# A fused gather-sum and MLP kernel: the three layers and the transposes of each step one quad earlier in TensorE's order

## Chip, cores and metric

The kernel runs on one NeuronCore of a Trainium2 chip. The metric is the device time of one execution in microseconds, the median of several. Everything is float32.

## The reference, cut to what matters

There are 12,500 nodes with 128 features (`x`) and 200,000 edges with 128 features. Edges are sorted by their destination `dst`; `src` takes no part in the result.

```python
h   = relu(layernorm(x))                                   # no affine part
agg = segment_sum(edge_attr, dst, num_segments=12500)      # [12500, 128]
u   = relu(concat([h, agg]) @ W1 + b1)
u   = relu(u @ W2 + b2)
y   = u @ W3 + b3
out = x + layernorm(y) * ln_w + ln_b
```

## The kernel before

**Units of work.** A chunk is 384 edges (128 partitions, 3 edges each), a quad is 4 chunks (1,536 edges, 768 KB), and there are 130 full quads and a tail chunk. A group is 384 nodes (3 per partition); there are 32 full groups and a last one of 212 nodes. A step handles four quads (k = 0 to 3) and one group; there are 31 steps, after six quads that run ahead (AHEAD = 6). All edges of a group must have been summed before its first layer needs the sums; step i computes group i after the quads up to 4i + 4 have been added.

**A quad.** SyncE loads it into one of eight slots of `ring` in two DMAs (L293), each reload waiting until the segment sum that used the slot is done. VectorE writes one-hot matrices for two quads at a time (`make_onehot`, L862). TensorE's `seg` (L422) multiplies one-hots and edges, 12 calls that show as 24 matmuls, into `part_ps`, two banks by turns. ScalarE copies the result to `part` (`copy_part`, L639). GpSimd builds a placement matrix (`placement`, L784), which may run one quad ahead of `put`. TensorE's `put` (L433) multiplies the two into `place_ps`; it handles the quad before the one just summed. VectorE's `add` (L938) adds that to `agg` at a base read from a table.

**A group.** VectorE takes statistics of x (`stats_x` L835, `mean_x` L843), ScalarE the root (`x_sqrt` L645), VectorE the reciprocal and shift (`scale_x` L850, `shift_x` L855), ScalarE writes h (`normalise` L653) and GpSimd adds ln_b to x (`bias_x` L792) once h is written. TensorE transposes h (`transpose_h` L442), ScalarE copies that to `h_t` (`copy_ht` L662). Layer 1 is a product of h (`layer1_x` L450) and one of the sums (`layer1_sums` L457, which waits for `added`); ScalarE's `relu1` (L669), then layer 2 (L467), `relu2` (L675), then layer 3 (L473), six matmuls into the single bank `y_ps`. VectorE empties it (`take_y` L943), takes statistics (`stats_y` L963, `mean_y` L971), centers in three instructions (`center_y` L979), and after ScalarE's `y_sqrt` (L681) does `scale_y` (L987) and `output` in three instructions (L997), and SyncE stores the group. `layer3(g)` waits for `y_evacuated`, which `take_y(g - 1)` signals.

**What sets the order.** Each engine runs its own program in order, written out by hand in a function `step` per engine; semaphores join them. The order in `step` is what the change edits, for TensorE, ScalarE and VectorE. GpSimd's step (`rows_of`, four placements, `bias_x(i + 1)`) and SyncE's (a load of x, four reloads) are untouched. The last two groups and the last quads are written out behind the loop on each engine (from `q, g = QUADS - 4, GROUPS - 2`). Most of the output stores are issued by SyncE only after its last load. A first part of the program checks that the fast path fits the data; this one always takes it.

Of the kernel before, what the change touches and what calls it, by code (L numbers as in the profile page):

```python
# [70 lines left out]
AHEAD = 6  # L71
# [5 lines left out]
def gnn_kernel(nc, x, dst, edges, w1, b1, w2, b2, w3, b3, lnw, lnb, out):  # L77
    assert GROUPS == 32 and QUADS == 4 * STEPS + AHEAD and LAST_P * LAST_PER == LAST_N and RC * RP == REST
    with ExitStack() as ctx:
# [73 lines left out]
        x_loaded = [sem("x_loaded_even"), sem("x_loaded_odd")]  # L153
# [116 lines left out]
        with nc.Block() as block:  # L270
# [113 lines left out]
            def _(pe):  # L384
# [75 lines left out]
                def layer1(g, sums=None):  # L460
                    layer1_x(g)
                    layer1_sums(g, sums)
# [32 lines left out]
                def fast():  # L495
                    pe.wait_ge(wts_loaded, WTS)
                    for q in range(AHEAD):
                        if q >= 2:
                            pe.wait_ge(part_copied, q - 1)
                            seg(q, q, LANDED, q // 2 + 1)  # L500
                        if q >= 1:
                            put(q - 1, q - 1, free=q >= 3)
                    transpose_h(0)

                    def step(i, par, pairs):


                        for k in range(4):
                            turn_q = 4 * par + AHEAD + k
                            q = 4 * i + AHEAD + k  # L510
                            seg(q, turn_q, LANDED * (pairs + turn_q // RING + 1),
                                2 * i + AHEAD // 2 + k // 2 + 1 if k % 2 == 0 else None)
                            put(q - 1, turn_q - 1)
                            if k == 0:
                                layer1(i, 4 * i + AHEAD - 1)
                            elif k == 1:
                                layer2(i)
                            elif k == 2:
                                layer3(i)
                            else:  # L520
                                transpose_h(i + 1)

                    step(0, 0, 0)
                    with pe.Fori(0, (STEPS - 3) // 2) as t:
                        step(2 * t + 1, 1, t)
                        step(2 * t + 2, 0, t + 1)
                    step(STEPS - 2, 1, (STEPS - 2) // 2)

                    q, g = QUADS - 4, GROUPS - 2

                    def loads_of(quad):
                        return LANDED * (quad // RING + 1)

                    layer1_x(g)
                    seg(q, q, loads_of(q), q // 2 + 1)
                    put(q - 1, q - 1)
                    layer1_sums(g, q - 1)
                    put(q, q)  # L540
                    transpose_h(g + 1)
                    seg(q + 1, q + 1, loads_of(q + 1))
                    layer2(g)
                    put(q + 1, q + 1)
                    layer1_x(g + 1)
                    seg(q + 2, q + 2, loads_of(q + 2), q // 2 + 2)
                    layer3(g)
                    put(q + 2, q + 2)
                    seg(q + 3, q + 3, loads_of(q + 3))
                    layer1_sums(g + 1, QUADS - 1)  # L550
                    put(q + 3, q + 3)
                    slot = QUADS % RING
                    pe.wait_ge(onehot_ready, QUADS // 2 + 1)
                    pe.wait_ge(edges_loaded[slot], loads_of(QUADS) - LANDED + 16)
                    for j in range(PER):
                        last = nc.tensor.matmul(part_ps[QUADS % 2][0:WIN, 0:D], onehot[:, (QUADS // 2) % 2, 0, j, :],
                                                ring[:, slot, j * D:(j + 1) * D], start=(j == 0), stop=(j == PER - 1))
                    last.then_inc(seg_done, 1)
                    layer2(g + 1)
                    layer1_x(LAST)  # L560
                    put(QUADS, QUADS, rows=WIN)
                    layer3_last_bias()
                    layer3(g + 1)
                    layer1_sums(LAST, QUADS + 1)
                    layer2(LAST)
                    layer3_last()
# [49 lines left out]
            def _(act):  # L616
# [71 lines left out]
                def fast():  # L688
                    act.wait_ge(wts_loaded, WTS)
                    for q in range(2):  # L690
                        copy_part(q, q)
                    x_sqrt(0)
                    normalise(0)
                    for q in range(2, AHEAD):
                        copy_part(q, q)
                    copy_ht(0)

                    def step(i, first=False, more_x=False):
                        q = 4 * i + AHEAD
                        copy_part(q, AHEAD)  # L700
                        relu1(i)
                        x_sqrt(i + 1)
                        copy_part(q + 1, AHEAD + 1)
                        relu2(i)
                        normalise(i + 1)
                        copy_part(q + 2, AHEAD + 2)
                        if not first:
                            y_sqrt(i - 1)
                        copy_part(q + 3, AHEAD + 3)
                        copy_ht(i + 1)  # L710
                        if more_x:
                            x_sqrt(i + 2)
                            normalise(i + 2)

                    step(0, first=True)
                    with act.Fori(1, STEPS - 2) as i:
                        step(i)
                    step(STEPS - 2, more_x=True)

                    q, g = QUADS - 4, GROUPS - 2  # L720
                    copy_part(q, q)
                    relu1(g)
                    copy_ht(g + 1)
                    copy_part(q + 1, q + 1)
                    relu2(g)
                    y_sqrt(g - 1)
                    copy_part(q + 2, q + 2)
                    copy_part(q + 3, q + 3)
                    relu1(g + 1)
                    y_sqrt(g)  # L730
                    copy_part(QUADS, QUADS, rows=WIN)
                    relu2(g + 1)
                    relu1(LAST)
                    relu2(LAST)
                    y_sqrt(g + 1)
                    act.wait_ge(y_centered, g + 2)
                    act.wait_ge(y_rstd_done, g + 2)
                    for j in range(PER):
                        nc.scalar.activation(z[:, j, :], z[:, j, :], ACT.Copy, scale=y_rstd[:, j:j + 1]).then_inc(z_scaled, 1)
                    y_sqrt(LAST)  # L740
                    act.wait_ge(full_out_ready, PER)
                    act.dma_start(group_rows(out, g + 1), xg(g + 1)).then_inc(stored, 16)
# [87 lines left out]
            def _(dve):  # L830
# [179 lines left out]
                def fast():  # L1010
# [8 lines left out]
                    base = bases(0, AHEAD - 1)  # L1019
# [8 lines left out]
                    def step(i, par, pairs, first=False, more_x=False):  # L1028

                        make_onehot(2 * i + 4, 0)
                        base = bases(4 * i + AHEAD - 1, 4)
                        q = 4 * i + AHEAD - 1
                        add(q, 1, base[0])
                        stats_x(i + 1, x_loaded[1 - par], 16 * (pairs + par) + 16)
                        if not first:
                            take_y(i - 1)
                        add(q + 1, 0, base[1])  # L1040
                        mean_x(i + 1)
                        if not first:
                            stats_y(i - 1)
                        scale_x(i + 1)
                        shift_x(i + 1)
                        if not first:
                            mean_y(i - 1)
                        add(q + 2, 1, base[2])
                        if not first:
                            center_y(i - 1)  # L1050
                        make_onehot(2 * i + 5, 1)
                        if more_x:
                            stats_x(i + 2, x_loaded[par], 16 * pairs + 32)
                            mean_x(i + 2)
                        add(q + 3, 0, base[3])
                        if more_x:
                            scale_x(i + 2)
                            shift_x(i + 2)
# [14 lines left out]
                    add(q - 1, q - 1, base[0])  # L1073
                    stats_y(g - 1)
                    mean_y(g - 1)
                    add(q, q, base[1])
                    center_y(g - 1)
                    make_onehot(q // 2 + 2, 1)
                    add(q + 1, q + 1, base[2])
                    scale_y(g - 1)  # L1080
                    output(g - 1)
                    add(q + 2, q + 2, base[3])
                    take_y(g)
                    stats_y(g)
                    mean_y(g)
                    center_y(g)
                    scale_y(g)
# [83 lines left out]
```

## Time and profile before

| | |
|---|---|
| median of 3 runs | 320.87 us (320.09 to 321.0) |
| the profiled execution | 320.3 us |
| its span in the profile | 318.4 us |
| TensorE matmul busy | 273.7 us |
| VectorE busy | 246.2 us |
| GpSimd busy | 179.5 us |
| ScalarE busy | 149.8 us |
| bytes moved by DMA | 116.49 MB, mean 366 GB/s |
| mean granted TensorE clock | 0.977 |

The span runs from the first to the last recorded event, the execution's own time has a little around it. Busy is the time in which an engine ran at least one data instruction. The shares are means over a start of some 30 us, 31 steps and a tail of some 20 us, and each of these has a limit of its own.

### The profile page before, as it was taken

To read this page: it belongs to the slowest core of one execution; us is meant where nothing else is said; L and a number is where in the kernel's file an instruction comes from. 1 tells how busy PE (TensorE), PEld (TensorE's weight loads), DVE (VectorE), ACT (ScalarE), POOL (GpSimd) and SP (SyncE) were. 2 spreads that over 40 slices of the span, in tenths; PEclk is the share of its full clock that TensorE was granted. 3 is DMA by queue.
4 is the path that set the end of the run, shared out by engine and by line. 5 is a ranking of instruction groups with operands and counts; after the bars stand their busy time and mean duration, and the time that the engine had idled before them with its cause. 6 is when DMAs were issued, how large, how long until landed. Compare 5 with 4: busy or idle time off the path is not lost.

```text
span 318.4 us, 12666 instructions
## 1 busy us (share of the span) xinstructions
PE 273.7 (86%) x3927; PEld 186.3 (58%) x3927; DVE 246.2 (77%) x944; ACT 149.8 (47%) x407; POOL 179.5 (56%) x208
## 2 busy tenths in 40 slices
PE   2959998998988787999888888898888888898991
PEld 0736666665655555666556565565556565566560
DVE  4946588988778787588787977777787977777984
ACT  1542555555444444455444555544445555545632
POOL 8636555666545565266565665555565665555531
PEclk9977999999999999899999999999999999999997
DMA  7999999999999999999999999999999999999994
GB/s 245 344 379 371 373 371 372 373 386 373 386 373 379 381 373 386 373 374 372 373 373 373 373 374 372 373 373 373 373 373 373 373 373 373 373 373 374 376 399 158
DMA packets 81534, 116.49 MB, mean 366 GB/s; under 512 B 5392, under 2 KB 81520, under 8 KB 81520
## 3 DMA queue, kind: packets, MB, share of 16 engines
q1 hardware_dynamic: 80506, 115.86, 103.3%
q10 hardware_dynamic: 1014, 0.46, 0.5%
q8 instruction: 7, 0.11, 0.1%
q14 instruction: 7, 0.06, 0.1%
HBM read 109.90 MB, written 6.40 MB: 365 GB/s over the span
## 4 chain that ended last, share of the span: by engine, by line
SPq 52%; PE 18%; DMA 13%; issue 10%; DVE 5%; ACT 0%; POOL 0%; POOLq 0%; DVEq 0%
SPq L293 43%; DMA ring<-in_edge_attr 12%; PE part_ps L422 7%; SPq L288 5%; PE place_ps L433 3%; PE hid_ps L450 2%; PE y_ps L473 2%; PE hid_ps L457 2%; PE hid_ps L467 1%; DMA dst_i<-in_dst 1%; SPq L316 1%; SPq L320 1%; DVE local L884 1%; DVE least L882 1%; DVE span L887 1%
## 5 line engine op out<-in xcount | busy, mean ns | idle before, releaser
L784 POOL TENSOR_SCALAR place<-iota,rows_at 128x128 f32<-128x128 f32 x131 | 105.3, 808 | 104.8 <-PE place_ps L433 96.0
L422 PE MATMUL part_ps<-ring,onehot 128*32 128x128 f32 x3120 | 114.3, 281 | 26.0 <-DMA ring<-in_edge_attr 25.0
L422 PEld LDWEIGHTS part_ps<-ring,onehot 128*32 128x32 f32 x3120 | 79.0, 111 | 71.8 <-issue 50.5
L938 DVE TENSOR_TENSOR agg<-place_ps,agg 128x128 f32 x131 | 38.0, 290 | 52.7 <-PE place_ps L433 50.9
L433 PE MATMUL place_ps<-place,part 128*128 128x128 f32 (+1 forms) x262 | 64.7, 330 | 2.6 <-POOL place L784 2.3
L792 POOL TENSOR_TENSOR xs<-xs,vecs 128x384 f32 (+2 forms) x33 | 54.9, 1664 | 19.3 <-ACT h L653 19.3
L862 DVE TENSOR_TENSOR onehot<-iota,local_t 128x768 f32<-128x768 f32 x66 | 63.5, 964 | 0.3 <-issue 0.3
L639 ACT ACTIVATE part<-part_ps 128x128 f32<-128x128 f32 x131 | 35.0, 268 | 48.4 <-PE part_ps L422 46.7
L433 PEld LDWEIGHTS place_ps<-place,part 128*128 128x128 f32 (+1 forms) x262 | 40.0, 191 | 29.3 <-issue 22.4
L653 ACT ACTIVATE h<-xs,x_shift,x_rstd 128x128 f32 (+2 forms) x98 | 41.3, 483 | 2.4 <-DVE x_shift L855 2.4
L669 ACT ACTIVATE hid<-hid_ps,b1s 128x384 f32<-128x384 f32 (+1 forms) x33 | 19.0, 577 | 46.2 <-PE hid_ps L457 46.2
L997 DVE SCALAR_TENSOR_TENSOR xs<-z,y_rstd,xs 128x128 f32 (+1 forms) x93 | 32.5, 401 | 4.1
L473 PE MATMUL y_ps<-w3s,hid 128*128 128x128 f32 x192 | 29.8, 291 | 0.0
L645 ACT ACTIVATE x_std<-x_mv,eps 128x3 f32<-128x3 f32 (+1 forms) x33 | 9.8, 297 | 41.0 <-DVE x_mv L843 41.0
L979 DVE SCALAR_TENSOR_TENSOR z<-y,y_mv,vecs 128x128 f32<-128x128 f32 x96 | 29.0, 355 | 0.1
L662 ACT ACTIVATE h_t<-ht_ps 128x384 f32<-128x384 f32 x32 | 22.3, 696 | 13.6 <-PE ht_ps L442 13.6
L450 PE MATMUL hid_ps<-h_t,w1x 128*128 128x384 f32 x64 | 26.7, 500 | 0.8 <-ACT h_t L662 0.8
L467 PE MATMUL hid_ps<-hid,w2s 128*128 128x384 f32 (+1 forms) x66 | 26.8, 487 | 0.5 <-ACT hid L669 0.5
L457 PE MATMUL hid_ps<-agg,w1a 128*128 (+2 forms) x66 | 26.5, 484 | 0.0
L473 PEld LDWEIGHTS y_ps<-w3s,hid 128*128 128x128 f32 x192 | 23.8, 191 | 1.4 <-issue 0.5
L835 DVE BATCH_NORM_STATS2 x_stats<-xs 128x6 f32 (+2 forms) x98 | 22.0, 279 | 0.8 <-DVE flag_i L924 0.8
L963 DVE BATCH_NORM_STATS2 y_stats<-y 128x6 f32<-128x128 f32 x96 | 20.8, 272 | 0.1
(86 smaller groups left out, 202.7 us busy)
## 6 DMA issues: line engine op xcount, KB each, us to landing
ring<-in_edge_attr SPq DMA_DIRECT2D x260, 384.0 KB, 9.2
xs<-in_x SPq DMA_DIRECT2D x32, 192.0 KB, 9.0
out_x<-xs SPq DMA_DIRECT2D x15, 384.0 KB
dst_i<-in_dst SPq DMA_DIRECT2D x1, 768.0 KB
ring<-in_edge_attr SPq DMA_DIRECT2D x1, 192.0 KB, 9.4
out_x<-xs SPq DMA_DIRECT2D x1, 192.0 KB
out_x<-xs ACTq DMA_DIRECT2D x1, 192.0 KB
xs<-in_x SPq DMA_DIRECT2D x1, 96.0 KB
```

The source lines that it names most:

```text
L293: sp.dma_start(ring_slot(slot)[:, k * HALF:(k + 1) * HALF, :], half_of_edges(q, k)).then_inc(edges_loaded[slot], 16)
L422: last = nc.tensor.matmul(part_ps[par_q % 2][s * WIN:(s + 1) * WIN, 0:D], onehot[:, oct_par, first + s, j, :], e[:, s, j * D:(j + 1) * D], ...
L433: nc.tensor.matmul(place_ps[par_q % 2][:, 0:P], part[0:rows, par_q % 2, :], place[0:rows, par_q % 2, :], start=True, stop=True).then_inc(p ...
L450: nc.tensor.matmul(hid1_ps[:, 0:n], w1x[:, :], t[:, :], start=True, stop=False)
L457: nc.tensor.matmul(hid1_ps[:, 0:n], w1a[:, :], agg[:, bass.ds(g * CHUNK, n)], start=False, stop=True).then_inc(hid1_done, 1)
L473: last = nc.tensor.matmul(y_ps[:, j * D:(j + 1) * D], hid2[:, j, :], w3s[:, :], start=True, stop=True)
L639: nc.scalar.activation(part[0:rows, par_q % 2, :], part_ps[par_q % 2][0:rows, 0:D], ACT.Copy).then_inc(part_copied, 1)
L653: last = nc.scalar.activation(h[0:rows, j, :], xg(g, j), ACT.Relu, bias=x_shift[0:rows, j:j + 1], scale=x_rstd[0:rows, j:j + 1])
L784: nc.gpsimd.tensor_scalar(place[:, par_q % 2, :], iota[:, 0:P], rows_at[:, k:k + 1], None, ALU.is_equal).then_inc(place_ready, 1)
L792: nc.gpsimd.tensor_tensor(v, v, lnbs[0:rows, :].unsqueeze(1).to_broadcast([rows, per, D]), ALU.add).then_inc(x_biased, 1)
L862: nc.vector.tensor_tensor(onehot[:, par % 2, :, :, :], iota[:, 0:WIN].unsqueeze(1).unsqueeze(1).to_broadcast([P, OCT, PER, WIN]), local_t[ ...
L938: nc.vector.tensor_tensor(v, place_ps[par_q % 2][:, 0:P], v, ALU.add).then_inc(added, 1)
```

## The change

On TensorE the whole of layer 1 comes ahead of the segment sum with k = 0, layer 2 takes the place behind k = 0, layer 3 that behind k = 1 and the transposes that behind k = 2; nothing follows k = 3. ScalarE and VectorE are put in an order that goes with it, and so are the hand-written last steps.

```diff
--- before.py
+++ after.py
@@ -508,16 +508,16 @@
                         for k in range(4):
                             turn_q = 4 * par + AHEAD + k
                             q = 4 * i + AHEAD + k
+                            if k == 0:
+                                layer1(i, 4 * i + AHEAD - 1)
                             seg(q, turn_q, LANDED * (pairs + turn_q // RING + 1),
                                 2 * i + AHEAD // 2 + k // 2 + 1 if k % 2 == 0 else None)
                             put(q - 1, turn_q - 1)
                             if k == 0:
-                                layer1(i, 4 * i + AHEAD - 1)
+                                layer2(i)
                             elif k == 1:
-                                layer2(i)
+                                layer3(i)
                             elif k == 2:
-                                layer3(i)
-                            else:
                                 transpose_h(i + 1)
 
                     step(0, 0, 0)
@@ -533,18 +533,17 @@
                     def loads_of(quad):
                         return LANDED * (quad // RING + 1)
 
-                    layer1_x(g)
+                    layer1(g, q - 1)
                     seg(q, q, loads_of(q), q // 2 + 1)
                     put(q - 1, q - 1)
-                    layer1_sums(g, q - 1)
+                    layer2(g)
+                    seg(q + 1, q + 1, loads_of(q + 1))
                     put(q, q)
+                    layer3(g)
                     transpose_h(g + 1)
-                    seg(q + 1, q + 1, loads_of(q + 1))
-                    layer2(g)
                     put(q + 1, q + 1)
+                    seg(q + 2, q + 2, loads_of(q + 2), q // 2 + 2)
                     layer1_x(g + 1)
-                    seg(q + 2, q + 2, loads_of(q + 2), q // 2 + 2)
-                    layer3(g)
                     put(q + 2, q + 2)
                     seg(q + 3, q + 3, loads_of(q + 3))
                     layer1_sums(g + 1, QUADS - 1)
@@ -697,17 +696,17 @@
 
                     def step(i, first=False, more_x=False):
                         q = 4 * i + AHEAD
+                        relu1(i)
                         copy_part(q, AHEAD)
-                        relu1(i)
                         x_sqrt(i + 1)
-                        copy_part(q + 1, AHEAD + 1)
                         relu2(i)
                         normalise(i + 1)
-                        copy_part(q + 2, AHEAD + 2)
+                        copy_part(q + 1, AHEAD + 1)
                         if not first:
                             y_sqrt(i - 1)
+                        copy_part(q + 2, AHEAD + 2)
+                        copy_ht(i + 1)
                         copy_part(q + 3, AHEAD + 3)
-                        copy_ht(i + 1)
                         if more_x:
                             x_sqrt(i + 2)
                             normalise(i + 2)
@@ -718,12 +717,12 @@
                     step(STEPS - 2, more_x=True)
 
                     q, g = QUADS - 4, GROUPS - 2
+                    relu1(g)
                     copy_part(q, q)
-                    relu1(g)
-                    copy_ht(g + 1)
-                    copy_part(q + 1, q + 1)
                     relu2(g)
                     y_sqrt(g - 1)
+                    copy_part(q + 1, q + 1)
+                    copy_ht(g + 1)
                     copy_part(q + 2, q + 2)
                     copy_part(q + 3, q + 3)
                     relu1(g + 1)
@@ -1030,29 +1029,28 @@
 
 
 
+                        stats_x(i + 1, x_loaded[1 - par], 16 * (pairs + par) + 16)
                         make_onehot(2 * i + 4, 0)
+                        mean_x(i + 1)
                         base = bases(4 * i + AHEAD - 1, 4)
                         q = 4 * i + AHEAD - 1
                         add(q, 1, base[0])
-                        stats_x(i + 1, x_loaded[1 - par], 16 * (pairs + par) + 16)
+                        scale_x(i + 1)
+                        shift_x(i + 1)
                         if not first:
                             take_y(i - 1)
                         add(q + 1, 0, base[1])
-                        mean_x(i + 1)
                         if not first:
                             stats_y(i - 1)
-                        scale_x(i + 1)
-                        shift_x(i + 1)
-                        if not first:
                             mean_y(i - 1)
                         add(q + 2, 1, base[2])
                         if not first:
                             center_y(i - 1)
                         make_onehot(2 * i + 5, 1)
+                        add(q + 3, 0, base[3])
                         if more_x:
                             stats_x(i + 2, x_loaded[par], 16 * pairs + 32)
                             mean_x(i + 2)
-                        add(q + 3, 0, base[3])
                         if more_x:
                             scale_x(i + 2)
                             shift_x(i + 2)
@@ -1073,15 +1071,15 @@
                     add(q - 1, q - 1, base[0])
                     stats_y(g - 1)
                     mean_y(g - 1)
+                    center_y(g - 1)
+                    scale_y(g - 1)
                     add(q, q, base[1])
-                    center_y(g - 1)
+                    output(g - 1)
                     make_onehot(q // 2 + 2, 1)
                     add(q + 1, q + 1, base[2])
-                    scale_y(g - 1)
-                    output(g - 1)
-                    add(q + 2, q + 2, base[3])
                     take_y(g)
                     stats_y(g)
+                    add(q + 2, q + 2, base[3])
                     mean_y(g)
                     center_y(g)
                     scale_y(g)
```

## Rows read from the trace of the kernel before

**Rows 1.** Page, part 1: busy time, share of the span and instructions of each engine

```profile
PE 273.7 (86%) x3927; PEld 186.3 (58%) x3927; DVE 246.2 (77%) x944; ACT 149.8 (47%) x407; POOL 179.5 (56%) x208
```

**Rows 2.** Page, part 4: the chain that ended last, by engine

```profile
SPq 52%; PE 18%; DMA 13%; issue 10%; DVE 5%; ACT 0%; POOL 0%; POOLq 0%; DVEq 0%
```

**Rows 3.** Timeline, TensorE: start, duration in us, line, operation, [idle before <- releaser]

```profile
198.11 0.86 PE L422 MATMUL part_ps<-ring,onehot 128*32 128x128 f32 x24 [1.04 <-DMA ring<-in_edge_attr]
...
284.20 0.93 PE L473 MATMUL y_ps<-w3s,hid 128*128 128x128 f32 x6
...
287.60 0.86 PE L422 MATMUL part_ps<-ring,onehot 128*32 128x128 f32 x24 [0.94 <-DMA ring<-in_edge_attr]
...
288.39 0.49 PE L433 MATMUL place_ps<-place,part 128*128 128x128 f32 x2
```

**Rows 4.** Timeline, TensorE, first steps and the tail's first product

```profile
29.17 0.49 PE L442 MATMUL ht_ps<-ident,h 128*128 128x128 f32 x3
...
30.71 0.81 PE L450 MATMUL hid_ps<-h_t,w1x 128*128 128x384 f32 x2
...
38.56 0.81 PE L450 MATMUL hid_ps<-h_t,w1x 128*128 128x384 f32 x2
...
296.31 0.91 PE L450 MATMUL hid_ps<-h_t,w1x 128*128 128x384 f32 x2 [0.78 <-ACT h_t L662]
```

**Rows 5.** Timeline, VectorE: links of the step's chain

```profile
33.72 0.30 DVE L843 BATCH_NORM_AGGREGATE x_mv<-x_stats 128x2 f32<-128x6 f32 x3
...
34.39 0.18 DVE L850 RECIPROCAL x_rstd<-x_std 128x3 f32<-128x3 f32 x1 [0.36 <-ACT x_std L645]
...
53.28 0.95 DVE L862 TENSOR_TENSOR onehot<-iota,local_t 128x768 f32<-128x768 f32 x1
...
54.15 0.28 DVE L938 TENSOR_TENSOR agg<-place_ps,agg 128x128 f32 x1
...
54.35 0.16 DVE L987 RECIPROCAL y_rstd<-y_std 128x3 f32<-128x3 f32 x1
...
55.70 0.96 DVE L862 TENSOR_TENSOR onehot<-iota,local_t 128x768 f32<-128x768 f32 x1 [0.16 <-issue]
...
57.36 0.54 DVE L943 TENSOR_TENSOR y<-y_ps,vecs 128x384 f32<-128x384 f32 x1
...
289.02 0.29 DVE L938 TENSOR_TENSOR agg<-place_ps,agg 128x128 f32 x1
```

**Rows 6.** Timeline of all engines around `bias_x` (L792), three places

```profile
50.49 0.49 PE L433 MATMUL place_ps<-place,part 128*128 128x128 f32 x2
...
51.19 0.60 POOL L784 TENSOR_SCALAR place<-iota,rows_at 128x128 f32<-128x128 f32 x1 [1.25 <-PE place_ps L433]
...
51.69 1.67 DVE L979 SCALAR_TENSOR_TENSOR z<-y,y_mv,vecs 128x128 f32<-128x128 f32 x3
...
52.22 1.00 POOL L792 TENSOR_TENSOR xs<-xs,vecs 128x384 f32 x1 [0.43 <-ACT h L653]
...
54.28 0.86 PE L422 MATMUL part_ps<-ring,onehot 128*32 128x128 f32 x24 [1.00 <-DVE onehot L862]
...
284.83 0.87 DVE L979 SCALAR_TENSOR_TENSOR z<-y,y_mv,vecs 128x128 f32<-128x128 f32 x3
...
285.58 1.85 POOL L792 TENSOR_TENSOR xs<-xs,vecs 128x384 f32 x1 [0.42 <-ACT h L653]
...
302.93 1.62 DVE L997 SCALAR_TENSOR_TENSOR xs<-z,y_rstd,xs 128x128 f32<-128x128 f32 x3
...
303.06 1.09 POOL L792 TENSOR_TENSOR xs<-xs,vecs 128x384 f32 x1
```

**Rows 7.** Timeline, the tail: VectorE and TensorE

```profile
296.35 0.29 DVE L938 TENSOR_TENSOR agg<-place_ps,agg 128x128 f32 x1
...
304.81 0.91 PE L457 MATMUL hid_ps<-agg,w1a 128*128 128x384 f32 x2
...
305.25 0.68 DVE L963 BATCH_NORM_STATS2 y_stats<-y 128x6 f32<-128x128 f32 x3
```

## The prediction

> **What bounds the kernel now.** I read the page from the top. TensorE is busy for 86% of the span and VectorE for 77% [rows 1], so neither is free and neither is obviously the bound. The chain that ended last settles it: 52% of it is SyncE's queue and 13% a load in flight [rows 2]. The kernel moves at the pace at which quads of edges land. TensorE's timeline shows this inside a step: it stops once per step, at the segment sum with k = 0, until the load lands, by 0.94 to 1.04 us [rows 3]. The ten steps between the two rows of that kind take 89.49 us, so the DMA's step is 8.95 us. With nothing to wait for TensorE's own step is shorter: the first products of steps 0 and 1 stand 38.56 - 30.71 = 7.85 us apart [rows 4]. A step thus has 1.1 us of slack, and the change is free in the loop only if no chain of waits round the loop becomes longer than 8.95 us. After the last landing this slack is gone, and the tail runs at the pace of TensorE and VectorE.
>
> **The change, part by part.** No instruction is added or removed; all move. No DMA moves on a queue of its own, but SyncE's reload waits for the segment sum that frees the slot, so whatever delays that sum delays a reload, and GpSimd's placements wait for `put`, so they follow it too.
>
> Layer 1 ahead of the segment sum: it waits for the addition of the quad put last. Its x product runs first and covers the 0.63 us from a put to the start of its addition (288.39 to 289.02) [rows 3, 5], if VectorE is free. Priced at nothing there; without that cover it is the wait below. In step 0 the cover for the copy of the transposes is gone too: transposes at 29.17, 0.49 of them, 0.78 until the product [rows 4], so layer 1 starts at 30.44.
>
> Layer 3 one quad earlier: this is the costly part. `y_ps` is one bank, so `layer3(i)` waits for `take_y(i - 1)`. Before, layer 3 came a quad later and `take_y` was one of VectorE's first operations in the step; now `take_y` stands behind `stats_x`, a one-hot, `mean_x`, an addition, `scale_x` (which waits for ScalarE's root) and `shift_x`. Behind the waiting layer 3 stand the next segment sum and the put whose quad VectorE needs next. That closes a ring: `take_y`, layer 3, segment sum k = 2, its put, addition, centering, one-hot, addition, output, next step's statistics, and `take_y` again.
>
> Its length, link by link:
> - `take_y` 0.54 and 0.05 to TensorE (the one-hot of 53.28 ends at 54.23 and TensorE goes on at 54.28): 0.59 [rows 5, 6].
> - Layer 3 to the segment sum: 0.93 less the usual overlap of 0.07, 0.86. Segment sum to put: 288.39 - 287.60 = 0.79 [rows 3].
> - From the put VectorE adds and centers; with nothing in the way that is 0.63 + 0.20 + (0.87 - 0.08) = 1.62 to the one-hot, 1.7 with the 0.1 that the addition is later in every other step [rows 5, 6].
> - One-hot to addition: 54.15 - 53.28 = 0.87 [rows 5].
> - Addition to the next step's `mean_x`: 54.15 to 57.36 is 3.21 and holds an addition, reciprocal, output, one-hot, addition and `stats_x`; less one addition (0.20) 3.01. A 0.16 idle piece of it [rows 5] need not recur: 2.85 to 3.01, I take 2.93.
> - `mean_x` to `scale_x` with the root between: 34.39 - 33.72 = 0.67; `scale_x` and `shift_x` 0.18 and about 0.16 [rows 5].
>
> Sum without any disturbance: 0.59 + 0.86 + 0.79 + 1.70 + 0.87 + 2.93 + 0.67 + 0.34 = 8.75 us. That is still under 8.95, by 0.2.
>
> **The disturbance.** GpSimd's `bias_x` now arrives at another moment. Its data are ready a quad earlier, as ScalarE's `normalise` moves up, so it follows at once upon the last placement. A placement starts 51.19 - 50.49 = 0.70 after the put and takes 0.60 [rows 6], and where `bias_x` had its data it started with no idle time before it (303.06), so it starts about 1.30 after the put. Before, it waited 0.42 more for `normalise` and came when the centering was ending: the row at 285.58 starts 0.75 after the centering's start, loses to the one-hot and takes 1.85 instead of 1.00, which costs VectorE nothing. That is the pattern of 28 steps [rows 6]. Now it arrives 0.3 to 0.46 after the centering's start, in the middle of its three pieces. The trace has two cases of that kind: at 52.22 the centering took 1.67 instead of 0.87 to 0.89 and TensorE then waited 1.00 for the one-hot, and at 303.06 the output took 1.62 [rows 6]. In both the rest of VectorE's pieces stood until GpSimd was through. By 52.22 the one-hot starts 53.28 - 52.22 = 1.06 after `bias_x`. So the link put to one-hot becomes 1.30 + 1.06 = 2.36 in place of 1.70, and the ring 8.75 + 0.66 = 9.41 us. The bounds: nothing (GpSimd loses, as in the 28 rows), 8.75; or two pieces held, another 0.26, 9.67. I take one piece, the nearer row.
>
> The Trainium skill, SBUF — State Buffer, section Who interferes with whom, says that a VectorE instruction with two SBUF inputs and a reading GpSimd instruction exclude each other, and that issue order decides who blocks. By that rule `bias_x` gets in behind the piece that is running and the sum is the longer one; a model that shared the bandwidth would leave it near the shorter. The trace agrees in the two cases, though at 52.22 the piece that lost is recorded 0.01 us ahead of the winner.
>
> **The sum.** Layer 1 of step 0 starts at 30.44 and the next at 38.29, 7.85 later, with put(8) just ahead of it at 37.9. Step 1 still runs at TensorE's pace, as there is no y of an earlier step to wait for until late: put(12) would stand at 45.8, and put(11) ahead of it by the transposes, a segment sum and a put (0.49, 0.79 and 0.49 less their overlaps, 1.5), at 44.3. Then 2.36 to the one-hot and 0.87: addition 12 at 47.5. The ring turns 28 times more: 47.5 + 28 x 9.41 = 311.0 for addition 124, which stood at 296.35 [rows 7]. The DMA, at 8.95, is no longer the bound. TensorE's two stops per step are no longer than the one of 1.04 after which a segment sum still took 0.86 [rows 3], so nothing is set down for its clock.
>
> The tail then belongs to VectorE. From addition 124 to the closing product of layer 1 for the last full group took 304.81 - 296.35 = 8.46 [rows 7]. The new order puts ahead of it `stats_x` and `mean_x` (about 1.05 net of the wait for the root that was there anyway) and `take_y` and `stats_y` (0.54 + 0.68 = 1.2): 10.7. So 321.7, and from there to the end as before, 318.4 - 304.8 = 13.6: a span of 335.3. The profiled execution took 320.3 for a span of 318.4, and the median is 0.57 above it: 335.3 + 1.9 + 0.6 = 337.8, say **337.5 us**.
>
> **The rivals.**
> A. The ring stays at 8.75 because GpSimd loses or the piece loses less. Then the DMA still sets the pace and only the tail counts: addition 124 at about 295.4, +10.7, +13.6, 319.7 in span, **322.2 us**. For it: 28 rows in which GpSimd lost. Against: none of those arrives with pieces of the centering left. It decides below 0.2 us of loss per step.
> B. The other side, faster. Layer 1 now runs while TensorE would wait at k = 0, and the tail no longer stops at 296.31 for the copied transposes (0.78) nor at 304.81 for an addition (0.28) [rows 4, 7]: 320.9 - 1.1 = **319.8 us**. This needs VectorE to deliver addition 128 a microsecond earlier than now. From 296.35 on VectorE has no slack to speak of and its order puts 2.3 us more ahead of it, so the loop must free more than that; nothing in the rows does.
> C. A ring between the two, where a loss of 0.3 to 0.4 gives 9.1 or so: 28 x 0.3 less, **329 us**. For two pieces held: 28 x 0.26 more, **345 us**.
> D. Gains and losses of the tail cancel and the loop stays at the DMA's pace: **320.9 us**. Nothing speaks for just this.
>
> **How the numbers follow.** About 0.3% (1 us) is what a measurement of this kernel can tell from no change. Chances: forecast 0.58, C 0.12 (0.05 of it the upper), A 0.15, B 0.10, D 0.05. Slower by over 0.3% 0.83 (forecast, C and nearly all of A), within 0.07, faster 0.10. The range must reach to A to hold eight in ten, and above takes 0.16 us per turn on the ring: 321.5 to 342. The forecast's own range is 332 to 342.
>
> **What would show it.** Right: the steps in the middle 9.3 to 9.5 us apart, no wait of TensorE for loads there, a wait ahead of the six products of layer 3 for `take_y` (about 0.5) and one ahead of layer 1's second product for the addition (about 1.0), the centering at 1.5 to 1.7 us with `bias_x` at 1.0, SyncE waiting for TensorE. Wrong: steps of 8.95, `bias_x` still at 1.85 and centering at 0.9 (A), or layer 1's closing product of the last full group before 304 (B). The tail part is wrong if the products after 321.7 - 335.3 take other than 13.6.

## The result, and the profile after

The changed kernel takes 337.53 us (median of 6 runs, 336.82 to 338.59) against 320.86 us: a ratio of 1.0525, 95% interval 1.0495 to 1.0554. The forecast was 337.5 us.

From the page of the kernel after: busy times (as [rows 1]), the chain by engine (as [rows 2]), and two of the groups of instructions that changed length (centering, `bias_x`).

```profile
PE 282.5 (84%) x3927; PEld 182.8 (54%) x3927; DVE 263.7 (79%) x944; ACT 156.1 (47%) x407; POOL 147.8 (44%) x208
...
PE 49%; DVE 25%; issue 5%; DVEq 2%; ACT 0%
...
L978 DVE SCALAR_TENSOR_TENSOR z<-y,y_mv,vecs 128x128 f32<-128x128 f32 x96 | 50.2, 574 | 0.2
...
L791 POOL TENSOR_TENSOR xs<-xs,vecs 128x384 f32 (+2 forms) x33 | 35.5, 1077 | 6.7 <-ACT h L652 6.7
```

SyncE's queue and the loads have left the chain; it alternates between TensorE and VectorE. The centering took 29.0 us in all before and takes 50.2, while `bias_x` fell from 54.9 to 35.5: time has moved from GpSimd, where it was free, to VectorE. Two other groups became shorter, the output (L997 before, 32.5 to 27.2) and GpSimd's placements (105.3 to 94.0), so VectorE is busy for 17.5 us more and not for 21.

Of the 17.2 us by which the span grew (318.4 to 335.6), 13.3 lie ahead of addition 124 (309.61 against 296.35 [rows 7]), 3.6 between it and layer 1's closing product, and 0.3 behind that.

The wait of SyncE's queue for the segment sums in the kernel after (engine, line <- what it waited for: us in total, times, longest):

```profile
SPq L293 <- PE part_ps L422: 66.0, 79, 2.0
```

Before, this row read 3.2 us. Reloads now wait for TensorE, not TensorE for loads.

One step in the kernel after, timeline of TensorE, VectorE and GpSimd (as [rows 3, 5, 6]):

```profile
231.67 0.49 PE L433 MATMUL place_ps<-place,part 128*128 128x128 f32 x2
...
235.36 0.91 PE L457 MATMUL hid_ps<-agg,w1a 128*128 x2 [1.01 <-DVE agg L937]
...
238.85 0.49 PE L433 MATMUL place_ps<-place,part 128*128 128x128 f32 x2
239.33 0.91 PE L473 MATMUL y_ps<-w3s,hid 128*128 128x128 f32 x6
...
240.96 0.49 PE L433 MATMUL place_ps<-place,part 128*128 128x128 f32 x2
```

```profile
232.50 1.64 DVE L978 SCALAR_TENSOR_TENSOR z<-y,y_mv,vecs 128x128 f32<-128x128 f32 x3
234.06 0.95 DVE L861 TENSOR_TENSOR onehot<-iota,local_t 128x768 f32<-128x768 f32 x1
234.93 0.28 DVE L937 TENSOR_TENSOR agg<-place_ps,agg 128x128 f32 x1
...
237.68 0.31 DVE L842 BATCH_NORM_AGGREGATE x_mv<-x_stats 128x2 f32<-128x6 f32 x3
...
238.64 0.55 DVE L942 TENSOR_TENSOR y<-y_ps,vecs 128x384 f32<-128x384 f32 x1
```

```profile
232.93 1.06 POOL L791 TENSOR_TENSOR xs<-xs,vecs 128x384 f32 x1
```

`bias_x` starts 232.93 - 231.67 = 1.26 after the put and 0.43 into the centering, which takes 1.64; the one-hot comes 1.13 after `bias_x`. The view of line 978 from 232 to 235 us gives the three pieces of that centering (shortest, median, longest in ns):

```profile
L978 DVE SCALAR_TENSOR_TENSOR z<-y,y_mv,vecs x3: 341/370/1084, 232.5 to 233.1; 128x128 f32<-128x128 f32 x3
```

One piece is held, the one that starts last, and two are not. From the put of one step to that of the next it is 240.96 - 231.67 = 9.29, and 9.41 for the step behind it, 9.35 on the mean. This path, which ends where it began one step later, is the ring. Layer 3 starts 239.33 - 238.85 = 0.48 after its put (an unhindered one takes 0.33) and 0.14 after `take_y` ends, so its own wait is 0.15; layer 1's second product waits 1.01.

### The profile page after: what moved, and what is told of

Same layout as the page of the kernel before. It is cut to its first block, busy times and chain, and to the rows that moved or that the text cites. A ratio compares the mean times of both kernels' runs of the same rounds, so it can differ in the third digit from the quotient of the medians.

```text
span 335.6 us, 12652 instructions
## 1 busy us (share of the span) xinstructions
PE 282.5 (84%) x3927; PEld 182.8 (54%) x3927; DVE 263.7 (79%) x944; ACT 156.1 (47%) x407; POOL 147.8 (44%) x208
## 4 chain that ended last, share of the span: by engine, by line
PE 49%; DVE 25%; issue 5%; DVEq 2%; ACT 0%
PE part_ps L422 19%; DVE z L978 11%; PE place_ps L433 10%; PE y_ps L473 8%; DVE onehot L861 8%; PE hid_ps L457 7%; PE hid_ps L467 5%; DVE agg L937 4%; DVE y_stats L962 1%; DVE xs L996 1%; DVEq L926 1%; DVE y L942 0%; DVEq L937 0%; DVEq L933 0%; DVEq L993 0%
## 5 line engine op out<-in xcount | busy, mean ns | idle before, releaser
L783 POOL TENSOR_SCALAR place<-iota,rows_at 128x128 f32<-128x128 f32 x131 | 94.0, 718 | 165.8 <-PE place_ps L433 157.0
L457 PE MATMUL hid_ps<-agg,w1a 128*128 (+2 forms) x66 | 29.5, 528 | 30.2 <-DVE agg L937 30.2
L978 DVE SCALAR_TENSOR_TENSOR z<-y,y_mv,vecs 128x128 f32<-128x128 f32 x96 | 50.2, 574 | 0.2
L791 POOL TENSOR_TENSOR xs<-xs,vecs 128x384 f32 (+2 forms) x33 | 35.5, 1077 | 6.7 <-ACT h L652 6.7
L457 PEld LDWEIGHTS hid_ps<-agg,w1a 128*128 128x128 f32 x66 | 9.9, 188 | 49.0 <-issue 44.6
L473 PE MATMUL y_ps<-w3s,hid 128*128 128x128 f32 x192 | 28.9, 286 | 2.1 <-DVE y L942 0.6
L996 DVE SCALAR_TENSOR_TENSOR xs<-z,y_rstd,xs 128x128 f32 (+1 forms) x93 | 27.2, 348 | 4.0
L661 ACT ACTIVATE h_t<-ht_ps 128x384 f32<-128x384 f32 x32 | 23.3, 727 | 13.4 <-PE ht_ps L442 13.4
```

The costliest lines, as they stand in the source:

```text
L457: nc.tensor.matmul(hid1_ps[:, 0:n], w1a[:, :], agg[:, bass.ds(g * CHUNK, n)], start=False, stop=True).then_inc(hid1_done, 1)
L473: last = nc.tensor.matmul(y_ps[:, j * D:(j + 1) * D], hid2[:, j, :], w3s[:, :], start=True, stop=True)
L783: nc.gpsimd.tensor_scalar(place[:, par_q % 2, :], iota[:, 0:P], rows_at[:, k:k + 1], None, ALU.is_equal).then_inc(place_ready, 1)
L791: nc.gpsimd.tensor_tensor(v, v, lnbs[0:rows, :].unsqueeze(1).to_broadcast([rows, per, D]), ALU.add).then_inc(x_biased, 1)
L978: last = nc.vector.scalar_tensor_tensor(z_of(g, j), y_of(g, j), y_mv[0:rows, j, 0:1], lnws[0:rows, :], ALU.subtract, ALU.mult)
```

## The experiments

Each is the kernel after, or before, with one edit. Times are medians; the kernel before took 320.3 to 320.6 us beside them.

**GpSimd alone: `bias_x` ahead of the last placement (order after).**

```diff
                         for k in range(4):
+                            if k == 3:
+                                bias_x(i + 1)
                             placement(4 * i + AHEAD + k, k, k, i + 2)
-                        bias_x(i + 1)
```

> The kernel after the change, with GpSimd's bias_x(i + 1) ahead of the step's last placement instead of behind it. It then starts while VectorE takes the statistics of y. No engine but GpSimd is edited. Theory 1: the centering falls from 1.64 to 0.87, both rings shrink by 0.77 to 8.6 and 8.5, under the 8.95 of the loads; TensorE waits for loads again, and the loop costs nothing: 323 us (the tail's extra stays). Rival (the order of TensorE and VectorE alone makes the steps long, the collision hides behind waits): steps stay at 9.3 and the time at 335 to 338 us.

Measured: 322.38 us, ratio 1.0049 (1.0026 to 1.0072). VectorE and TensorE in its timeline:

```profile
231.09 0.90 DVE L979 SCALAR_TENSOR_TENSOR z<-y,y_mv,vecs 128x128 f32<-128x128 f32 x3
...
240.46 0.86 PE L422 MATMUL part_ps<-ring,onehot 128*32 128x128 f32 x24 [0.42 <-DMA ring<-in_edge_attr]
```

The centering is back at 0.90, and from 133 us on the steps are 8.96 and TensorE waits for loads again. Moving one GpSimd instruction takes 15 of the 17 us away. Ahead of 133 us no load is waited for, and the ring can be seen without the collision. TensorE there:

```profile
61.08 0.91 PE L473 MATMUL y_ps<-w3s,hid 128*128 128x128 f32 x6 [0.18 <-DVE y L943]
65.66 0.91 PE L457 MATMUL hid_ps<-agg,w1a 128*128 x2 [0.28 <-DVE agg L938]
```

Both waits are there, and the steps between 45 and 133 us are 8.55 to 8.9, most of them under 8.7: the ring is closed, and shorter than the pace of the loads.

**The collision alone, in the order before.** `bias_x` one step late, so that it has its data and follows the last placement at once.

```diff
                         placement(q, q, q, 1, free=False)
-                    bias_x(0)
...
                             placement(4 * i + AHEAD + k, k, k, i + 2)
-                        bias_x(i + 1)
+                        bias_x(i)
...
                     g = GROUPS - 1
+                    bias_x(g)
```

> The kernel before the change, all orders of TensorE, ScalarE and VectorE untouched; only GpSimd's bias_x is put one step later (bias_x(i) in step i, where its data have long been ready), so that it follows the last placement at once and meets the centering. Theory 1 (the cost needs both, the collision and the ring closed by the new order): the centering shows 1.6 us in every step, but in the old order the one-hot behind it is needed only by the segment sum that waits for a load anyway (ready about 287.4 against a landing at 287.6), so steps stay at 8.95 and the time is 320.5 to 322 us. Rival (0.77 us more of VectorE per step is the cost, whatever the order): 325 to 340 us.

Measured: 321.43 us, ratio 1.0032 (1.002 to 1.0043).

```profile
284.61 1.71 DVE L979 SCALAR_TENSOR_TENSOR z<-y,y_mv,vecs 128x128 f32<-128x128 f32 x3
284.90 1.00 POOL L792 TENSOR_TENSOR xs<-xs,vecs 128x384 f32 x1
286.24 0.95 DVE L862 TENSOR_TENSOR onehot<-iota,local_t 128x768 f32<-128x768 f32 x1
287.37 0.86 PE L422 MATMUL part_ps<-ring,onehot 128*32 128x128 f32 x24 [0.94 <-DMA ring<-in_edge_attr]
```

The collision is there in full, 1.61 to 1.72 in every step. From 180 us on the loads pace the steps, 8.93 to 8.99 by TensorE's waits; most of the earlier ones are paced by the one-hot and are 8.55 to 8.75, which is shorter still. The one-hot ends at 287.19, just before the load for which the segment sum waits. The loss lies in the tail, where nothing covers: the segment sum at 287.37 is no later than before (287.60), addition 124 comes at 296.87 and the closing product at 306.86, against 296.35 and 304.81. (The profiled execution took 322.6 us, the slowest of its eight, so these differences are above the 1 us of the medians.) So the order alone costs 2 us (the experiment before), the collision alone 1, and both together 17.

**Layer 3 alone put back (order after).**

```diff
-                            elif k == 1:
-                                layer3(i)
                             elif k == 2:
+                                layer3(i)
                                 transpose_h(i + 1)
```

> The kernel after the change, with layer 3 alone put back in the loop, to behind the put of k = 2 and ahead of the transposes; layer 1 still ahead of the first segment sum, bias_x still meeting the centering. Theory 1: layer 3 and its waits (for take_y, and for relu2 behind the root) no longer stand between put k = 1 and put k = 2. The ring that is left, put k = 2, addition, centering (1.6), one-hot, addition, layer 1, is 3.67 + 4.61 = 8.3 us, under 8.95: the loads pace the loop and the time is 322 to 324 us. Rival (layer 1's wait behind the collision is enough by itself): steps of 9.1 or more, 331 us or more.

Measured: 321.72 us, ratio 1.0038 (1.0024 to 1.0053). Its timeline:

```profile
230.59 1.65 DVE L977 SCALAR_TENSOR_TENSOR z<-y,y_mv,vecs 128x128 f32<-128x128 f32 x3
...
233.45 0.91 PE L457 MATMUL hid_ps<-agg,w1a 128*128 x2 [0.35 <-DVE agg L936]
...
237.91 0.86 PE L422 MATMUL part_ps<-ring,onehot 128*32 128x128 f32 x24 [0.49 <-DMA ring<-in_edge_attr]
```

The collision stays at 1.65, layer 1 still waits for its addition (0.35), and yet the loads pace the loop at 8.96 from 130 us on (8.66 to 8.86 in most steps before). Layer 3 between the puts of k = 1 and k = 2 is needed for the loss.

**`take_y` first in VectorE's step (order after).**

```diff
+                        if not first:
+                            take_y(i - 1)
                         stats_x(i + 1, x_loaded[1 - par], 16 * (pairs + par) + 16)
...
                         shift_x(i + 1)
-                        if not first:
-                            take_y(i - 1)
```

> The kernel after the change, with take_y(i - 1) made VectorE's first operation of the loop's step; TensorE's order is untouched. Theory 1 (the ring of the prediction: take_y, layer 3, segment sum, put, centering, one-hot, addition, output, statistics, take_y): this ring is broken. What is left is a second ring that the profile after shows and the prediction did not sum: put(4i + 7), addition, centering, one-hot, addition 4i + 8, closing product of layer 1, segment sum, put, layer 2, segment sum, put, layer 3, segment sum, put. From 231.67 to 240.96 it takes 9.29 with layer 3 starting 0.48 after its put; with the bare 0.33 it is 9.14. So steps of 9.1 us and a time of 337.5 - 28 x 0.22 = 331 us. If the first ring were all that matters: steps of 8.95 and 323 us. Rival (layer 1's wait alone sets the pace, layer 3 is innocent): no change, 337 us.

Measured: 335.79 us, ratio 1.0479 (1.0438 to 1.0521): 2 us gained, not 6, and the 331 us expected were missed. ScalarE, VectorE and TensorE in its timeline:

```profile
209.24 0.31 DVE L842 BATCH_NORM_AGGREGATE x_mv<-x_stats 128x2 f32<-128x6 f32 x3
```

```profile
209.58 0.30 ACT L644 ACTIVATE x_std<-x_mv,eps 128x3 f32<-128x3 f32 x1 [1.08 <-DVE x_mv L842]
209.78 0.56 ACT L674 ACTIVATE hid<-hid_ps,b2s 128x384 f32<-128x384 f32 x1
```

```profile
210.40 0.94 PE L473 MATMUL y_ps<-w3s,hid 128*128 128x128 f32 x6
```

`take_y` is out of the way (it starts at 207.33), but it has pushed `mean_x` back by half a microsecond. ScalarE's `x_sqrt` waits for `mean_x`, `relu2` stands behind `x_sqrt`, and layer 3 needs `relu2`: it still starts 0.46 after its put. The ring closes through ScalarE instead, and steps are 9.28 to 9.38. The expectation had put down a bare 0.33 there and overlooked this.

**Layer 1 put back (order after), without and with `take_y` first.**

```diff
-                            if k == 0:
-                                layer1(i, 4 * i + AHEAD - 1)
                             seg(q, turn_q, LANDED * (pairs + turn_q // RING + 1),
...
                             if k == 0:
+                                layer1(i, 4 * i + AHEAD - 1)
                                 layer2(i)
...
-                        relu1(i)
                         copy_part(q, AHEAD)
+                        relu1(i)
```

> The kernel after the change, with layer 1 in the loop put back behind the first segment sum and its put, right ahead of layer 2 (ScalarE's copy of the quad ahead of relu1 to match); layer 3 and the transposes stay early. Theory 1 (ring through take_y and layer 3): TensorE gains slack ahead of layer 3 and loses it there, steps stay at 9.3 and the time at 335 to 338 us. Rival (layer 1's wait for the addition sets the pace): the wait of 1.0 per step is gone, steps fall to 8.95 and the time to 323 us.

> The edits of the first and third kernel together: take_y first in VectorE's step and layer 1 behind the first put. Theory 1 with the second ring: neither ring is closed, the loads pace the loop at 8.95 although the collision of bias_x and centering stays (centering still 1.6), and the time is 323 us. If the collision by itself costs (VectorE as the bound): VectorE's own work with it is about 8.3 to 8.7 per step, so still 323; 330 or more would say that a third chain exists.

Measured: 359.59 us, ratio 1.1199 (1.1148 to 1.125), and 360.03 us. Both theories missed. TensorE in the first of the two:

```profile
208.72 0.49 PE L433 MATMUL place_ps<-place,part 128*128 128x128 f32 x2
...
212.11 0.86 PE L422 MATMUL part_ps<-ring,onehot 128*32 128x128 f32 x24 [1.37 <-DVE onehot L860]
...
215.35 0.91 PE L467 MATMUL hid_ps<-hid,w2s 128*128 128x384 f32 x2 [0.67 <-ACT hid L667]
```

Layer 2 directly behind layer 1 waits 0.67 for `relu1`, and that wait, layer 1 itself and layer 3 now all stand between the put of k = 2 and the next one, behind a segment sum that waits 1.37 for the one-hot of the collided centering. The ring is 10.15 us (208.72 to 218.87). On the rival, that layer 1's wait for the addition sets the pace by itself, these two runs say nothing, as the edit made a stall of its own; the run with layer 3 back speaks against it, since that wait and the collision are still there and the time is 321.7. What the two runs show is that the way from the centering back to TensorE runs over the one-hot as well as over the addition.

**Tail and loop apart.** Loop orders of one kernel with the hand-written last steps of the other, on all three engines.

> Loop orders of after, hand-written last steps of before. Theory 1: steps stay at 9.35, addition 124 stands near 309.6, and the old tail saves what the new one costs VectorE: 8.5 to 9 us from there to the closing product of layer 1 in place of 12.0, so 3 us less: 334.5 us. If the tail's order is without effect: 337.5 us.

> Loop orders of before, hand-written last steps of after. Theory 1: the loop stays with the loads, the new tail costs VectorE about 1.2 us (take_y and stats_y of group 30 ahead of addition 128) and up to 1.1 us of waiting for the table of bases: 321.5 to 323.5 us. Rival B of the prediction (the new tail is shorter where TensorE sets it): 319.5 us.

Measured: loop of after with the old tail 336.72 us, ratio 1.0518 (1.0485 to 1.0551); loop of before with the new tail 320.70 us, ratio 1.0012 (1.0 to 1.0025). Both expectations were missed. The old tail was to give 3 us back and gives 0.8, which the scatter of the two kernels covers (335.77 to 337.7 against 336.82 to 338.59 us); the new tail was to cost 1 to 3 us and costs 0.3. In its trace the stretch from addition 124 to the closing product is 305.02 - 296.19 = 8.83 against 8.46: `take_y` and `stats_y` are added there, and the output that met `bias_x` (1.62 [rows 6]) takes 0.87. So the loss needs the loop's new order, whichever of the two tails follows. Yet the tail of the kernel after is longer. Its VectorE:

```profile
309.61 0.28 DVE L937 TENSOR_TENSOR agg<-place_ps,agg 128x128 f32 x1
...
312.60 1.04 DVE L861 TENSOR_TENSOR onehot<-iota,local_t 128x768 f32<-128x768 f32 x1
...
315.35 0.56 DVE L942 TENSOR_TENSOR y<-y_ps,vecs 128x384 f32<-128x384 f32 x1 [1.71 <-issue]
...
321.32 0.28 DVE L937 TENSOR_TENSOR agg<-place_ps,agg 128x128 f32 x1
```

In the 1.71 us nothing is waited for but the engine's own loads of the bases, here as the view of line 926 from 310 us on gives them:

```profile
L926 DVEq TENSOR_LOAD <-base_i x2: 1027/1724/2420, 311.8 to 314.3; - x2
```

The kernel with the old tail behind the new loop shows the same idle time (1.69) and needs 320.37 - 308.83 = 11.5 for the stretch, not the 8.5 to 9 expected; in the kernels whose loop is paced by the loads these two take 0.76 to 1.06.

**One constant: stores inside the loop (order after).**

```diff
-STORED_EARLY = 8
+STORED_EARLY = 26
```

> The kernel after the change with one constant changed, STORED_EARLY 8 to 26: the stores that SyncE issued in a row behind its last load go out inside the loop. It asks why VectorE's two loads of bases in the tail take 2.42 and 1.03 us in the kernels with the long step and 0.76 to 1.06 in the others. If the row of stores in flight is the cause: both near 0.8, the idle time of 1.71 ahead of take_y gone and 1.7 us less in the tail, against up to 3 us more in the loop, where loads and stores together need about 9.4 per step: 336 to 339 us. If it is not: 2.4 and 1.0 as before and 338 to 340 us.

Measured: 336.01 us, ratio 1.0468 (1.0443 to 1.0493). The same view and VectorE's timeline:

```profile
L926 DVEq TENSOR_LOAD <-base_i x2: 750/754/759, 313.3 to 314.1; - x2
```

```profile
315.03 0.55 DVE L942 TENSOR_TENSOR y<-y_ps,vecs 128x384 f32<-128x384 f32 x1
```

Both loads are short again and the idle time is gone, and the steps stay at 9.35. The long ones go with the row of stores. How the stores reach them was not tried, and the kernel before, with its own row of stores issued at the same place in the program, had 0.76 for both; this stays open.

**The last steps rewritten, on top of the early `bias_x`.**

```diff
                     relu1(g)
+                    x_sqrt(g + 1)
                     copy_part(q, q)
+                    normalise(g + 1)
                     relu2(g)
...
-                    center_y(g - 1)
-                    scale_y(g - 1)
                     add(q, q, base[1])
-                    output(g - 1)
+                    center_y(g - 1)
                     make_onehot(q // 2 + 2, 1)
                     add(q + 1, q + 1, base[2])
+                    add(q + 2, q + 2, base[3])
+                    scale_y(g - 1)
+                    output(g - 1)
                     take_y(g)
                     stats_y(g)
-                    add(q + 2, q + 2, base[3])
                     mean_y(g)
```

(`y_sqrt(g - 1)` goes behind the next copy; ScalarE's last loop step gives up `x_sqrt` and `normalise` of the group ahead, which are the two added lines; and VectorE's last loop step has `scale_x` and `shift_x` of that group behind `output`.)

> The orders of after with bias_x ahead of the last placement (as in the second kernel), and the last steps rewritten: ScalarE's relu1 of group 30 ahead of normalise of group 31, VectorE's additions 127 and 128 ahead of output(29), take_y(30) and stats_y(30). Theory 1: the loop stays at 8.95, addition 128, at 306.43 in the second kernel's trace, comes after 2.5 us less of VectorE's work, near 304, where TensorE asks for it; the closing product of layer 1 moves from 306.75 to 304.3 and the time from 322.4 to 319.9 us, at or just under before. If the tail is set by something else: 322 us.

Measured: 320.30 us, ratio 0.9998 (0.9988 to 1.0008). As expected against 322.38, and a tie with the kernel before. Its TensorE:

```profile
304.42 0.91 PE L457 MATMUL hid_ps<-agg,w1a 128*128 128x384 f32 x2
```

The closing product is 0.39 earlier than the 304.81 of before [rows 7], and the rest takes 14.0 instead of 13.6. No kernel of the study beats the one before by more than a measurement can tell.

## Why the prediction was right

**The ring.** The mechanism was named, and the runs show what it needs: with no collision 322.4, with layer 3 back 321.7, with the collision in the old order 321.4, with all of them together 337.5. That rival A would have needed GpSimd to lose is borne out by the first of these: its loop is rival A's, with addition 124 at 295.56 against the 295.4 computed for A, and its time 322.38 against 322.2. Of the two bounds of the collision the prediction chose the right one, one piece held.

One link is not needed as it was named. The wait of layer 3 for `take_y`, put at about 0.5, was 0.15, and with `take_y` out of the way the steps were 9.28 to 9.38 all the same, as `mean_x`, `x_sqrt` and `relu2` hold layer 3 at nearly the same time. The wait for the addition ahead of layer 1's second product was foreseen at about 1.0 and was 1.01, but not that it closes a ring of its own: put, centering, one-hot, addition, layer 1, and from there along TensorE through layer 3 to the next such put. Without any wait of layer 3 this one would be 9.29 - 0.15 = 9.14, an estimate that no run tested, and still over 8.95. In it layer 3 costs by the 0.8 of its own work, not by what it waits for, and less those 0.8 it is 8.3, under 8.95. The run with layer 3 back is under 8.95 too, though not at 8.3: its early steps are 8.66 to 8.86, with up to 0.38 in which the put waits for ScalarE's copy.

**Its length.** 9.41 was summed and 9.35 measured. Within it two links were off by more than the total: `take_y` to layer 3 is 0.69 (0.55 and 0.14), not 0.59, and the addition to the next step's `mean_x` is 237.68 - 234.93 = 2.75, not 2.93. Put to one-hot was 2.36 in the sum and is 2.39 (231.67 to 234.06). The ring without the collision was summed at 8.75 and shows as 8.55 to 8.7 where the early `bias_x` keeps ahead of the loads' pace, so the collision added some 0.7 (9.35 less 8.62, the mean of 8.55 and 8.69), near the 0.66 of the sum.

**The start.** Layer 1 of step 0 was put at 30.44 and stands at 30.40; the next at 38.29 and stands at 38.28; put 11 at 44.3 and stands at 44.38; addition 12 at 47.5 and comes at 47.64.

**Loop and tail.** Here two errors cancelled. Addition 124 was put at 311.0 and came at 309.6, as the ring was 0.06 shorter than summed, 28 times. The stretch from there to the closing product was put at 10.7 and took 321.65 - 309.61 = 12.0. The sum that failed is 8.46 + 1.05 + 1.2. It left out 1.71 us in which VectorE waits for its loads of bases, which the kernel before hid completely, and the 0.74 by which the output became shorter, as `bias_x` no longer meets it (1.62 to 0.88). From the closing product to the end 13.95 was measured against 13.6. The sum of span, 335.3 against 335.6, is better than its parts, and that is luck.

**Rival B** fell where the prediction said: VectorE, not TensorE, sets the tail. With the new tail behind the old loop there is no gain (320.70), and only with the early `bias_x` and once VectorE's additions were moved ahead in the tail did the product come earlier than before.

The Trainium skill, SBUF — State Buffer, section Who interferes with whom, has issue order decide who blocks. The runs agree for the collision itself: `bias_x` issued 0.43 or 0.29 into the centering holds the piece behind, and issued while the statistics of y run (229.34 in the kernel with the early `bias_x`) it leaves them at 0.67.

## What to carry to other kernels

When work is moved to an earlier place in an in-order engine, follow each wait it brings until it closes on itself, and compare the ring's length with the pace of the bound, not with the engine's busy time: here a ring of about 8.6 us under 8.95 us of loads was free, and one of 9.35 was not. Ask too what becomes ready earlier on the engines that were not edited: a GpSimd operation that no longer waited 0.4 us for its data met VectorE at another moment, and 15 us hung on it. Where a stall hides behind a load, its cost is zero until the ring around it reaches the load's pace.

## What the runs showed of the hardware that was not expected

Three instructions of 128 by 128 values, each of which reads two tensors from SBUF (the centering), run in 0.87 to 0.90 together, and in 1.61 to 1.72 when GpSimd's addition of 384 columns arrives ahead of the third; the GpSimd instruction itself takes 1.00 to 1.17 then, and 1.68 to 1.85 in the 28 steps of before where it arrives at the end of the centering and a long one-hot goes first.

Who wins within 0.1 us of a boundary can't be read off the starts. In the kernel before, at 52.22, `bias_x` is recorded 0.01 behind the third piece and goes first; at 285.58 it is recorded 0.04 ahead of this one-hot and takes 1.85 all the same [rows 6]:

```profile
285.62 0.95 DVE L862 TENSOR_TENSOR onehot<-iota,local_t 128x768 f32<-128x768 f32 x1
```

VectorE's register loads from a table in SBUF took 0.76 us each in one tail and 2.42 and 1.03 in another, with the same instructions; with the stores moved into the loop they took 0.76 and 0.75. The idle time of 1.71 stands only ahead of `take_y` with the long pair; with the short pair of the kernel before VectorE shows none there.
